# ScalarE turns two score tiles in one operation of 1024 columns, and the probabilities lie in twelve tiles in turn

## The reference, cut to what matters

```python
q = _split_heads(hidden_states @ w_q, HEADS)       # (8, 20, 512, 16)
k = _split_heads(text @ w_k, HEADS)                # (8, 20, 1593, 16)
v = _split_heads(text @ w_v, HEADS)
out_text = _merge_heads(_sdpa(q, k, v))            # softmax(q k / 4) v
out_ip = _merge_heads(_sdpa(q, k_ip, v_ip, mask=mask_ip))   # 8 keys
out = (out_text + out_ip) @ w_out + b_out + residual
```

## Time and profile before

| what | value |
|---|---|
| median of 3 runs | 1841.28 us (1838.55 to 1843.44) |
| profiled execution | 1848.91 us, span 1847.0 us |
| TensorE busy | 1811.4 us, 98% |
| VectorE busy | 1332.3 us, 72% |
| ScalarE busy | 1185.7 us, 64% |
| granted TensorE clock, mean | 0.993 |

### The profile page before, as it was taken

How to read it: one execution, slowest core, us unless ns; L and a number is a source line. 1 busy time by engine, 2 the same in 40 slices (tenths; PEclk the granted TensorE clock), 3 DMA queues, 4 the chain that set the end, 5 groups by cost and what they waited for, 6 DMA issues and landing times.

```text
span 1847.0 us, 41069 instructions
## 1 busy us (share of the span) xinstructions
PE 1811.4 (98%) x16856; PEld 718.8 (39%) x16856; DVE 1332.3 (72%) x1787; ACT 1185.7 (64%) x2340; POOL 382.6 (21%) x508
## 2 busy tenths in 40 slices
PE   8999999999999999999999999999999999999988
PEld 3333333433344343433344333343333433434332
DVE  6777777778767787677876777777777777767871
ACT  1276666666666666666666666666666666666766
POOL 5112222211122121122121221112122122221000
PEclk9999999999999999999999999999999999999989
DMA  7555334363344434355453464435544364343410
GB/s 226 102 92 160 67 77 92 73 164 73 74 106 116 106 71 86 94 139 102 79 99 75 141 103 77 97 69 144 94 77 96 72 155 85 74 95 74 77 30 26
DMA packets 103806, 178.16 MB, mean 96 GB/s; under 512 B 42933, under 2 KB 71270, under 8 KB 103618
## 3 DMA queue, kind: packets, MB, share of 16 engines
q1 hardware_dynamic: 82658, 134.12, 37.3%
q0 software_dynamic: 18944, 40.10, 6.9%
q10 hardware_dynamic: 2016, 1.31, 0.2%
HBM read 117.63 MB, written 48.98 MB: 90 GB/s over the span
## 4 chain that ended last, share of the span: by engine, by line
PE 93%; DMA 2%; DVE 2%; SPq 1%; ACT 1%; issue 1%; POOL 0%; ACTq 0%; DVEq 0%; POOLq 0%
PE pv_bank L800 27%; PE max_bank L727 20%; PE work_bank L582 12%; PE exp_bank L784 12%; PE work_bank L604 11%; PE work_bank L627 3%; PE work_bank L593 2%; PE max_bank L745 2%; PE exp_bank L788 1%; DVE tile_max L1069 1%; DMA o_t<-o_sum 1%; SPq L475 1%; ACT probs L978 1%; PE work_bank L658 1%; PE work_bank L611 1%
## 5 line engine op out<-in xcount | busy, mean ns | idle before, releaser
L978 ACT ACTIVATE probs<-exp_bank 128x512 f32<-128x512 f32 x1908 | 1002.0, 599 | 417.3 <-PE exp_bank L784 410.2
L1069 DVE TENSOR_REDUCE tile_max<-max_bank 128x2 f32<-128x1024 f32 x632 | 773.4, 1224 | 400.5 <-PE max_bank L727 395.5
L727 PE MATMUL max_bank<-k_stack,q_stack 48*128 48x512 f32 x1896 | 567.9, 469 | 7.4 <-DVE tile_max L1069 7.3
L800 PE MATMUL pv_bank<-probs,v_ones 128*17 128x512 f32 x3840 | 518.1, 603 | 0.1
L1071 DVE TENSOR_REDUCE tile_max<-max_bank 128x1 f32<-128x512 f32 x632 | 430.2, 681 | 2.7 <-PE max_bank L727 2.7
L784 PE MATMUL exp_bank<-q_stack,k_stack 50*128 50x512 f32 x1908 | 415.9, 403 | 4.0 <-DMA q_stack<-neg_rows 2.7
L727 PEld LDWEIGHTS max_bank<-k_stack,q_stack 48*128 48x128 f32 x1896 | 234.0, 185 | 409.8 <-issue 269.6
L784 PEld LDWEIGHTS exp_bank<-q_stack,k_stack 50*128 50x128 f32 x1908 | 240.0, 188 | 63.2 <-ACT probs L978 47.2
L582 PE MATMUL work_bank<-ctxt,wk 128*32 128x400 f32 x2528 | 253.5, 506 | 7.6 <-DMA wk<-in_w_k 5.5
L604 PE MATMUL work_bank<-wv,ctxt 128*32 128x320 f32 x3040 | 254.0, 435 | 0.0
L604 PEld LDWEIGHTS work_bank<-wv,ctxt 128*32 128x32 f32 x3040 | 93.8, 109 | 163.1 <-issue 100.3
(11 more groups left out here) (124 smaller groups left out, 832.3 us busy)
## 6 DMA issues: line engine op xcount, KB each, us to landing
k_stack<-scratch_k SPq DMA_DIRECT2D x234, 199.2 KB, 6.9
scratch_k<-k_parts SPq DMA_DIRECT2D x80, 400.0 KB, 4.6
ctxt<-in_ctx_t POOLq DMA_DIRECT2D x28, 800.0 KB, 11.1
q_stack<-scratch_q SPq DMA_DIRECT2D x240, 64.0 KB, 2.3
scratch_q<-q_parts SPq DMA_DIRECT2D x80, 128.0 KB, 5.7
r_wide<-scratch_r POOLq DMA_DIRECT2D x39, 256.0 KB, 5.1
xres<-in_x SPq DMA_DIRECT2D x8, 640.0 KB, 9.0
out<-xres SPq DMA_DIRECT2D x32, 160.0 KB, 1.9
```

The source lines that it names most:

```text
L727: nc.tensor.matmul(round_place(n, r)[:, k, :], exact(q_stack[stack, slot, c, t * 128:(t + 1) * 128]), exact(k_stack[stack, slot, c, chunk ...
L800: last = nc.tensor.matmul(pv_bank[h * 32:h * 32 + VW, :], v_ones[:, v_slot(b, kt), head * VW:(head + 1) * VW], p, start=(kt == 0), stop=(k ...
L978: nc.scalar.activation(dst, exp_place(group_no, at), ACT.Exp, scale=SCALE).then_inc(probs_ready, 1)
L1069: nc.vector.reduce_max(flat[:, at:at + 2], place[:, 0:2, :], AX.X).then_inc(max_taken, 1)
```

## The change

ScalarE takes the first two tiles of a visit in one operation over banks 0 and 1 of exp_bank, 1024 columns, and adds two to probs_ready at its end. The third tile, and all tiles of the last group, keep an operation of their own. So that the results of a pair lie side by side, the tiles of `probs` are no longer laid by key tile and head but in the order in which they are made, twelve in turn over all groups, the tail tiles among them. Where the first tile of a visit would fall on the last of the twelve places, the visit's tiles are made one by one. Every tile waits for the multiplication that read the tile twelve before it.

```diff
-PROB_RING = 3
+PROB_RING = 12
...
-        probs = sb("probs", [128, PROB_RING, GH, S])
-        probs_tail = sb("probs_tail", [128, GH // 2, S])
+        probs = sb("probs", [128, PROB_RING, S])
...
+        def probs_place(n, at):
+            return probs[:, (n * EXPS + at) % PROB_RING, :]
+
+        def pv_of(tile):
+            n, at = tile // EXPS, tile % EXPS
+            return n * KT + at // GH + 1
...
-                    p = probs[:, kt % PROB_RING, h, :] if kt < FULL else probs_tail[:, side_of(h)[1], :]
+                    p = probs_place(group_no, kt * GH + (HEADS_IN_TURN.index(h) if kt < FULL else side_of(h)[1]))
...
+            def exp_wait(group_no, at):
+                tile = group_no * EXPS + at - PROB_RING
+                act.wait_ge(scores_ready, group_no * EXPS + at + 1)
+                if tile >= 0 and (tile == 0 or pv_of(tile) != pv_of(tile - 1)):
+                    act.wait_ge(pv_done, pv_of(tile))
+
             def exp_tile(group_no, at):
-                act.wait_ge(scores_ready, group_no * EXPS + at + 1)
...
+                exp_wait(group_no, at)
+                nc.scalar.activation(probs_place(group_no, at), exp_place(group_no, at), ACT.Exp, scale=SCALE).then_inc(probs_ready, 1)
+
+            def exp_turns(group_no, v):
+                tiles = exp_turn(group_no, v)
+                first = (group_no * EXPS + tiles[0]) % PROB_RING if tiles else 0
+                if group_no < B * NG - 1 and first < PROB_RING - 1:
+                    for at in tiles[:2]:
+                        exp_wait(group_no, at)
+                    nc.scalar.activation(probs[:, first:first + 2, :], exp_bank[:, 0:2, :], ACT.Exp, scale=SCALE).then_inc(probs_ready, 2)
+                    tiles = tiles[2:]
+                for at in tiles:
+                    exp_tile(group_no, at)
...
-                        for at in exp_turn(group_no, v):
-                            exp_tile(group_no, at)
+                        exp_turns(group_no, v)
```

More of the change, by code:

```diff
@@ L273, in cross_attention @@
         ip_sum = sb("ip_sum", [128, QT, HEADS])
-        early = probs[:, :, :, :].rearrange("p a h n -> p (a h n)")
+        early = probs[:, :, :].rearrange("p a n -> p (a n)")
         wk_ip = early[:, 0:CT * D].rearrange("p (c n) -> p c n", c=CT)
@@ L962, in negative_copy @@
                                   neg_rows[side * (rows // SIDES):(side + 1) * (rows // SIDES), :]).then_inc(neg_loaded, 16)
-            def exp_tile(group_no, at):
-                act.wait_ge(scores_ready, group_no * EXPS + at + 1)
[L966 to L978, removed]
+            def exp_wait(group_no, at):
[3 more added lines that the diff above has]
+                    act.wait_ge(pv_done, pv_of(tile))
+            def exp_tile(group_no, at):
+                exp_wait(group_no, at)
[10 more added lines that the diff above has]
+                    exp_tile(group_no, at)
             def o_copy(group_no):
```

## The result

The changed kernel takes 1854.62 us (median of 6 runs, 1849.58 to 1857.3) against 1843.2: a ratio of 1.0062, interval 1.0046 to 1.0078. It is slower, by 11 us. The forecast was no change. Four executions in the last set of experiments took far longer than the rest (the kernel before 1873 and 4236 us, w1 9616, w3 4653) and count in no ratio; the last of them is w3's profiled one, so nothing is read from w3's trace.

The account below looks back on a forecast made before the run. TensorE was taken as the bound, busy 1811.4 of 1847.0 us with 93% of the chain. The terms -0.35 - 0.15 + 0.9 summed to +0.4 us, giving 1841.7 us, no change, range 1833 to 1850.

Parts of the forecast that it names:

- ScalarE's saving is off the path in the short visits: Visits without a piece of projection: third score tile's weights load 0.05 us earlier, max tile beside it does not; gain 0.
- VectorE's gate: Short visits: max tile's weights wait for VectorE's last reduction until 910.48, 0.04 us behind ScalarE's gate for the third score tile.
- the length of a pair: ScalarE's 1024-column exponential: 0.60 + 0.43 = 1.03 us, from 0.84 to 0.85 ns a column.
- the 0.92 us to the third: ScalarE's third exponential starts 0.92 us after the pair's start, against 0.97 before, so 0.05 us earlier.
- the counts: 611 pairs replace 1222 operations of 512 columns; ScalarE's instructions fall from 2340 to 1729.
- When the pair starts: Start of a visit: waiting for two score tiles costs 0 to 0.01 us; waits taken as 0, bound +0.06 us.
- Where the pair is late: Tail tiles at a group's end: next group's first score weights 0.10 us late at nine places, 0.9 us lost.
- The ring: Twelve tiles in turn for probs: the places' waits for earlier multiplications cost 0.
- The rivals: Alternatives to no change (70%): faster, waits on ScalarE set the pace, 15%; slower, the pair is dear, 10%.
- the slower rival: Two-bank restart or waits' dispatch delays the third exponential at 128 places: 10 us at +0.12, 18 at worst; 10%.
- The Trainium skill's rule: Rule against merging: forecast held it agrees at the tail tiles and would change nothing at the other visits.

Follow-up runs that it names:

- w1: The kernel before with two places for a group's outputs (o_sum), so ScalarE's copy does not wait for SyncE's transfers: 0.9961 of the kernel before, 1834.1 us.
- w3: The changed kernel with one wait per pair, tail tiles one by one and two places for the outputs: 0.9965 of the kernel before, 1834.9 us.
- x2: The changed kernel's ring of twelve tiles in turn, but no pairs, every tile with its own operation: 1.0003 of the kernel before.
- y2: The changed kernel with only the two tail tiles of visit 16 as a pair, with one wait: 1.0023 of the kernel before.
- y5: The changed kernel without pairs; in visit 16 the second tail tile's operation adds two, so both are released together: 1.0039 of the kernel before.
- y3: The changed kernel, doubled waits kept, with the tail tiles of visit 16 one by one: 1.0014 of the kernel before.
- w0: The changed kernel measured once more, for a second trace: 1.0049 of the kernel before, 1850.3 us.

## Why the prediction was wrong, step by step

- *That ScalarE's saving is off the path in the short visits*: right. VectorE's gate held the third slot, w3 against w1 shows no gain, and the length of a pair (1.03 us forecast, 1.025 measured), the 0.92 us to the third, and the counts came as worked out.
- *When the pair starts*: this step failed. I took 0 from two modelled ends that lay 0.01 us apart, with 0.06 as the bound for the waits, and took it that the first wait stays on the operation. It is 0.11 to 0.17: 0.03 for the second tile's later addition, 0.06 for the first wait, which the pair no longer carries itself, and 0.02 to 0.08 for the second. That turned 0.05 us won behind a pair into 0.05 to 0.11 lost, and cost visit 14 its 0.06 to 0.10.
- *Where the pair is late*: the place was right and the size nearly so. The next weights came 0.24 us later and not 0.10, the score tiles behind them 0.13, 1.1 us in all against a forecast of 0.9. That a late release delays nothing else was the second failure, and the larger in time. It went with a load of instructions on SyncE's issue in every second batch (that the one moved the other is argued, as said under *Open* below), in front of the only long wait of the loop, which I had read and used only for its 0.05 us of gain.
- *The ring*: right, x2.
- *The rivals*: the slower rival had its sign and its place, the start of the pair, but put the price on 128 short visits. With the third exponential 0.05 to 0.11 us later it would have been 1 to 9 us; most of these visits show no loss, since VectorE's gate in the same slot leaves 0.00 to 0.02. The 11 us are 4 to 5 of steady lateness elsewhere (of which the visits' medians name 2 to 3) and about 6 to 7 of the stall and its clock.
- *The Trainium skill's rule* that breaking operations up may let work finish sooner where ScalarE isn't saturated (Perfetto Trace Analysis, "Optimizing Scalar/DVE Operations"): the runs agree with it more than I did. I gave it the tail tiles alone and at face value, 0.9 us; y2 and y5 put 0.2 to 0.4% on them.

*Open*: that reading ahead is what moves the load is argued from y5 and the positions of the loads, not shown. Why 7 of the 29 longer stalls have no half clock behind them is open too; y5's trace has it behind all four, the kernel before behind one or none. And y2 and y3 do not add up exactly (0.23% and 0.14% against 0.62% together, 0.49% in w0), though their intervals allow it.

## What to carry to other kernels

Merging two operations of an engine that is not the bound won nothing here, and it makes the later input and the later release the rule for both tiles. Price the start of the merged operation by its waits: count the semaphore instructions that will stand ahead of it, and note that here an operation that adds two to a semaphore carried no wait of its own. Before a release is moved later, look for the longest wait of the loop and ask what else would fall into it. Here the larger gain lay in that wait itself: a second place for the outputs took 0.4% off.

## What the runs showed of the hardware

- A load of 16 KB of TensorE's instructions that started between 0.04 us before and 0.18 us after the start of SyncE's issue of a transfer stretched it from 0.59 us to 1.2 to 1.8 us (14 places); one that started 0.1 to 0.3 us before it, to 0.9 to 1.6 us; one that started 0.5 to 0.8 us before it, to at most 1.3 us, and at some places not at all.
- An exponential of ScalarE that carried its wait itself started 0.02 us after the addition it waited for; behind one semaphore instruction it was 0.07 to 0.08 us, with two waits in it 0.10, and behind two such instructions 0.16. All 611 operations that added two to a semaphore carried no wait of their own, nor did y5's 39.
- Two score tiles side by side on the two halves of the rows have modelled ends 0.01 us apart; their additions to the semaphore came 0.03 us apart.
- TensorE's granted clock fell to 0.50 (1.2 GHz) for 3.4 or 6.8 us behind 22 of 29 stalls of 1.21 to 2.13 us, and behind none of 76 stalls of 0.84 to 1.05 us.
- 64 semaphore instructions ahead of the first matmul moved its start from 5.4 to 12.2 us, 244 of them to 31.6 us: 0.11 us each.
